# The last normalisation pass of an attention and deformable-convolution kernel: where the second pass over eight results finds its data, and when it is loaded

## What is computed

```python
x = x + attention(group_norm(x))            # 8 heads of 48, 1024 tokens, softmax, projection
x = x + deform(group_norm(x))               # below

offset = clip(conv(x, off_w, off_b), -8, 8)     # 3x3
mask   = 2 * sigmoid(conv(x, mask_w, mask_b))   # 3x3
y      = bilinear samples of x at 9 shifted taps, times mask, times proj_w, plus proj_b
mean, var = y.mean(axis=(0, 2, 3)), y.var(axis=(0, 2, 3))   # over all 8 images
return gelu((y - mean) * rsqrt(var + 1e-5) * gamma + beta)
```

## Time and profile before

| | us |
| --- | --- |
| median of 3 runs | 3541.97 (3540.9 to 3545.35) |
| profiled execution | 3541.39 |
| its span in the trace | 3539.5 |
| PE busy | 3257.9 (92% of the span) |
| DVE busy | 2309.0 (65%) |
| ACT busy | 1672.5 (47%) |
| POOL busy | 1288.1 (36%) |

### The profile page before, as it was taken

One profiled execution on the slowest core, in us unless ns is written; L12 is line 12 of the kernel. 1 busy time (PEld: TensorE's weight loads), 2 busy tenths in 40 slices (PEclk: granted clock), 3 DMA queues, 4 the chain that ended last, 5 costly groups with the idle time before them and its releaser, 6 DMA issues. The chain is left out here.

```text
span 3539.5 us, 87588 instructions
## 1 busy us (share of the span) xinstructions
PE 3257.9 (92%) x33434; PEld 1904.8 (54%) x33434; DVE 2309.0 (65%) x3770; ACT 1672.5 (47%) x2700; POOL 1288.1 (36%) x1183
## 2 busy tenths in 40 slices
PE   5899999999999999999999999999999999997991
PEld 3265555555555555555556555555555555554660
DVE  5976677766766576766767667676676666765443
ACT  4274344544455443744437444464445544363443
POOL 0162334523343332622327133362334423262430
PEclk9799999999999999999999999999999999998995
DMA  4000000000001000000000000000000100001007
GB/s 139 19 2 37 19 1 21 20 19 19 2 22 37 2 19 3 21 37 1 20 21 3 37 19 2 21 2 37 19 1 22 38 1 1 2 21 72 1 1 321
DMA packets 12167, 97.59 MB, mean 28 GB/s; under 512 B 2813, under 2 KB 2941, under 8 KB 5008
## 3 DMA queue, kind: packets, MB, share of 16 engines
q1 hardware_dynamic: 9504, 67.40, 5.1%
q0 software_dynamic: 1152, 12.58, 0.8%
q10 hardware_dynamic: 1008, 11.01, 0.7%
HBM read 56.26 MB, written 34.60 MB: 26 GB/s over the span
## 5 line engine op out<-in xcount | busy, mean ns | idle before, releaser
L1612 PE MATMUL R<-P,WALL 128*128 128x512 f16 x3888 | 980.5, 378 | 0.3 <-issue 0.3
L634 POOL TENSOR_TENSOR PL<-P 128x1024 f16<-128x1024 f32 x256 | 583.0, 2282 | 544.1 <-ACT P L809 541.9
L1051 DVE TENSOR_REDUCE MXP<-G 128x1 f32<-128x512 f32 x926 | 630.7, 688 | 154.4 <-PE G L1368 149.6
L1591 PE MATMUL R<-MHL,XB 128*128 128x240 f16 (+14 forms) x7776 | 719.8, 234 | 2.4 <-DVE P L1282 2.4
L671 POOL TENSOR_TENSOR MHL<-M,MHL 128x280 f16<-128x280 f32 (+2 forms) x576 | 364.8, 635 | 796.3 <-ACT MHL L905 795.1
L809 ACT ACTIVATE P<-R 128x1024 f32<-128x1024 f32 x512 | 521.4, 1023 | 223.7 <-PE R L1413 222.8
L1591 PEld LDWEIGHTS R<-MHL,XB 128*128 128x128 f16 x7776 | 571.1, 98 | 102.5 <-DVE P L1282 2.7
L1612 PEld LDWEIGHTS R<-P,WALL 128*128 128x128 f16 x3888 | 377.9, 98 | 396.7 <-issue 0.5
L1123 DVE TENSOR_TENSOR PL<-P 128x1024 f16<-128x1024 f32 x256 | 463.4, 1812 | 150.8 <-ACT P L809 150.6
L1413 PE MATMUL R<-QK 48*128 48x512 f16 (+1 forms) x3072 | 435.1, 392 | 37.5 <-issue 22.9
L1431 PEld LDWEIGHTS R<-VS,P 128*128 128x128 bf16 x4096 | 322.1, 97 | 196.1 <-issue 155.2
(11 more groups left out here) (146 smaller groups left out, 3535.8 us busy)
## 6 DMA issues: line engine op xcount, KB each, us to landing
XA<-x SPq DMA_DIRECT2D x8, 1536.0 KB, 6.6
X<-x SPq DMA_DIRECT2D x8, 1536.0 KB, 6.8
x_scratch<-X SPq DMA_DIRECT2D x7, 1536.0 KB, 5.8
y_scratch<-XP ACTq DMA_DIRECT2D x7, 1536.0 KB, 5.1
WALL<-y_scratch SPq DMA_DIRECT2D x6, 1536.0 KB, 14.8
out<-WALL POOLq DMA_DIRECT2D x6, 1536.0 KB, 10.9
QK<-x_scratch SPq DMA_DIRECT2D x4, 1536.0 KB, 17.4
P<-wd SPq DMA_DIRECT2D x9, 576.0 KB, 4.9
```

Source lines behind the costliest of these rows:

```text
L634: pool.tensor_tensor(PL[:, s % P_BUFS, :], P32[:, s % P_BUFS, :], high_view(s), ALU.subtract).then_inc(p_low_pool, 1)
L1051: dve.reduce_max(MXP[:, name[1] % 2, n // 2, n % 2:n % 2 + 1], chunk(sec, name)[:, :], AX.X).then_inc(dve_read, 1)
L1591: last = pe.matmul(out, XT[:, x_part, g * BOX_Y + r, t * 128:(t + 1) * 128], MHL[:, m_part, o + at:o + at + (hi - lo) * (x1 - x0)], start= ...
L1612: last = pe.matmul(R6[:, CT + ct, :], WALL[:, w:w + 128], PHL[:, u % 2, part // 2, t, :], start=(u % TAPS == 0 and n < CT), stop=(u % TAPS ...
```

## The change

x1 of all k from 1 to 7 is loaded at about 3224 us, except the last third of the last one, which goes to the first tile of `X1` and waits for the first addition. For this, x1 of 5, 6 and 7 gets places in what the last image no longer needs: the rest of `QK4` and the V weights in `WALL`, `QZ` and `WP`, `WQK` (made flat, `WQKF`) and `X1`.

y of k = 1 and 2 is loaded when `taps_used` is raised, with the convolution of unit 15, after which the weights under these two places are not read again. y of k = 3, 4, 5 and 6 is loaded when `y_full` says that TensorE is through; 3 in `WALL`, the others in `XB`, `P32`, and `PL` with `MHL`. y of k = 7 goes into `YS` after the first result's store. VectorE raises `added` for each tile instead of for each result. GpSimd stores results 0 to 6 as before (6 in two pieces, as its place has two) and result 7 tile by tile.

```diff
+        X_AT = [[X1F], [places(QKF, 0)], [places(QKF, 2 * CT * PIX)], [XR.rearrange("p t n -> p (t n)")],
+                [places(VS[:, :, :, :].rearrange("p q h d -> p (q h d)"), 0)],
+                [places(QKF, 4 * CT * PIX, 2), places(WALL, WVO, 1)], [places(QZF, 0, 2), places(WPF, 0, 1)],
+                [places(WQKF[:, :], 0, 2), X1F[:, 0:PIX]]]
+        Y_AT_END = [[YSF], [places(WALL, 0)], [places(WALL, 4 * CT * PIX)], [places(WALL, 2 * CT * PIX)],
+                    [places(XB[:, :, :, :].rearrange("p a t n -> p (a t n)"), 0)],
+                    [P32[:, 0:CT, :].rearrange("p t n -> p (t n)")], [places(PLF, 0, 2), places(MHLF, 0, 1)], [YSF]]
...
             x1_done(BATCH - 1, True)
-            for k in range(1, min(XS, BATCH)):
-                sp.dma_start(XF(k), x1_d[FINAL[k], :, :]).then_inc(xf_in[k % XS], 16)
-            sp.wait_ge(y_stats, BATCH)
-            if BATCH > 1:
-                sp.wait_ge(y_out, BATCH * 16)
             for k in range(1, BATCH):
-                if k >= 4:
-                    sp.wait_ge(out_done[k % 4], 16 * (k // 4))
-                sp.dma_start(YF(k), y_d[FINAL[k], :, :]).then_inc(yf_in[k % 4], 16)
-                if k >= XS:
-                    sp.wait_ge(added, k - XS + 1)
-                    sp.dma_start(XF(k), x1_d[FINAL[k], :, :]).then_inc(xf_in[k % XS], 16)
+                final_x(k, pieces_of(X_AT[k])[:1 if k == BATCH - 1 else None])
+            sp.wait_ge(y_out, 16 * 3)
+            sp.wait_ge(taps_used, 1)
+            for k in (1, 2):
+                final_y(k)
+            sp.wait_ge(y_out, BATCH * 16)
+            sp.wait_ge(y_full, 2 * BATCH)
+            for k in range(3, BATCH - 1):
+                final_y(k)
+            sp.wait_ge(added, CT)
+            final_x(BATCH - 1, pieces_of(X_AT[BATCH - 1])[1:])
+            sp.wait_ge(out_done[0], 16)
+            final_y(BATCH - 1)
...
+            for k in range(BATCH - 1):
+                pool.wait_ge(added, (k + 1) * CT)
+                for a, cols in pieces_of(Y_AT_END[k]):
+                    pool.dma_start(out[FINAL[k], :, cols], a).then_inc(out_done[k], 16)
+            k = BATCH - 1
+            for t in range(CT):
+                pool.wait_ge(added, k * CT + t + 1)
+                pool.dma_start(out[FINAL[k], :, t * PIX:(t + 1) * PIX], final_tile(Y_AT_END[k], t)).then_inc(out_done[k], 16)
             for k in range(BATCH):
-                pool.wait_ge(added, k + 1)
-                pool.dma_start(out[FINAL[k], :, :], YF(k)).then_inc(out_done[k % 4], 16)
-            for k in range(min(4, BATCH)):
-                pool.wait_ge(out_done[k], 16 * len(range(k, BATCH, 4)))
+                pool.wait_ge(out_done[k], 16 * (CT if k == BATCH - 1 else len(Y_AT_END[k])))
...
-                last.then_inc(added, 1)
+                    dve.tensor_tensor(y, y, final_tile(X_AT[k], t), ALU.add).then_inc(added, 1)
...
                         if u % TAPS == TAPS - 1 and end == CONVS:
                             last.then_inc(y_full, 1)
+                        if final and u == UNITS - 3 and end == CONVS:
+                            last.then_inc(taps_used, 1)
```

More of the change, by code:

```diff
@@ L315, in build @@
         WALL = sb("WALL", [128, (2 * TAPS + 2) * TAPW], fp16)
-        WQK = sb("WQK", [128, 2, CT, 2 * PAIRS, QK_COLS], fp16)
+        WQKF = sb("WQK", [128, 2 * CT * 2 * PAIRS * QK_COLS], fp16)
+        WQK = WQKF[:, :].rearrange("p (a t m n) -> p a t m n", a=2, t=CT, n=QK_COLS)
         WP = sb("WP", [128, 2, CT, CH], fp16)
@@ L437, in build @@
         bn_ready = sem("bn_ready")
-        yf_in = [sem(f"yf_in{n}") for n in range(4)]
-        xf_in = [sem(f"xf_in{n}") for n in range(5)]
+        taps_used = sem("taps_used")
+        yf_in = [sem(f"yf_in{n}") for n in range(BATCH)]
+        xf_in = [sem(f"xf_in{n}") for n in range(BATCH)]
         gelu_done = sem("gelu_done")
         added = sem("added")
-        out_done = [sem(f"out_done{n}") for n in range(4)]
+        out_done = [sem(f"out_done{n}") for n in range(BATCH)]
         count_of = {"F": chunk_full, "A": act_read, "D": dve_read}
@@ L472, in build, with places, pieces_of, final_tile @@
         QKF = QK4[:, :, :, :].rearrange("p a i n -> p (a i n)")
[L473 to L476, removed]
+        X1F, YSF = [a.rearrange("p t n -> p (t n)") for a in (X1[:, :, :], YS[:, :, :])]
         FINAL = [BATCH - 1] + list(range(BATCH - 1))
[L482 to L490, removed]
+        def places(a, first, tiles=CT):
+            return a[:, first:first + 2 * tiles * PIX].bitcast(fp32)
+        WPF = WP[:, :, :, :].rearrange("p a t n -> p (a t n)")
+        QZF, MHLF = QZ[:, :, :, :].rearrange("p a d n -> p (a d n)"), MHL[:, :, :].rearrange("p a n -> p (a n)")
+        X_AT = [[X1F], [places(QKF, 0)], [places(QKF, 2 * CT * PIX)], [XR.rearrange("p t n -> p (t n)")],
[5 more added lines that the diff above has]
+                    [P32[:, 0:CT, :].rearrange("p t n -> p (t n)")], [places(PLF, 0, 2), places(MHLF, 0, 1)], [YSF]]
+        def pieces_of(areas):
+            out, t = [], 0
+            for a in areas:
+                n = a.shape[1] // PIX
+                out.append((a, slice(t * PIX, (t + n) * PIX)))
+                t += n
+            return out
+        def final_tile(areas, t):
+            for a, cols in pieces_of(areas):
+                if cols.start <= t * PIX < cols.stop:
+                    return a[:, t * PIX - cols.start:(t + 1) * PIX - cols.start]
         SELF = SEL[:, :, :].rearrange("p a n -> p (a n)")
@@ L593, in _, with final_x, final_y @@
             x1_done(BATCH - 1, True)
-            for k in range(1, min(XS, BATCH)):
-                sp.dma_start(XF(k), x1_d[FINAL[k], :, :]).then_inc(xf_in[k % XS], 16)
-            sp.wait_ge(y_stats, BATCH)
-            if BATCH > 1:
-                sp.wait_ge(y_out, BATCH * 16)
-            for k in range(1, BATCH):
-                if k >= 4:
-                    sp.wait_ge(out_done[k % 4], 16 * (k // 4))
-                sp.dma_start(YF(k), y_d[FINAL[k], :, :]).then_inc(yf_in[k % 4], 16)
-                if k >= XS:
-                    sp.wait_ge(added, k - XS + 1)
-                    sp.dma_start(XF(k), x1_d[FINAL[k], :, :]).then_inc(xf_in[k % XS], 16)
+            def final_x(k, pieces):
+                for a, cols in pieces:
+                    sp.dma_start(a, x1_d[FINAL[k], :, cols]).then_inc(xf_in[k], 16)
+            def final_y(k):
+                for a, cols in pieces_of(Y_AT_END[k]):
+                    sp.dma_start(a, y_d[FINAL[k], :, cols]).then_inc(yf_in[k], 16)
+            for k in range(1, BATCH):
+                final_x(k, pieces_of(X_AT[k])[:1 if k == BATCH - 1 else None])
[11 more added lines that the diff above has]
+            final_y(BATCH - 1)
         @block.gpsimd
@@ L959, in _ @@
                 if k > 0:
-                    act.wait_ge(yf_in[k % 4], 16 * ((k - 1) // 4 + 1) if k % 4 else 16 * (k // 4))
+                    act.wait_ge(yf_in[k], 16 * len(Y_AT_END[k]))
                 for t in range(CT):
-                    y = YF(k)[:, t * PIX:(t + 1) * PIX]
+                    y = final_tile(Y_AT_END[k], t)
                     act.activation(y, y, ACT.Gelu, bias=BSC[:, 3, t:t + 1], scale=BSC[:, 2, t:t + 1]).then_inc(gelu_done, 1)
@@ L1315, in _ @@
                 if k > 0:
-                    dve.wait_ge(xf_in[k % XS], 16 * ((k - 1) // XS + 1) if k % XS else 16 * (k // XS))
+                    dve.wait_ge(xf_in[k], 16 * len(X_AT[k]))
                 for t in range(CT):
-                    y = YF(k)[:, t * PIX:(t + 1) * PIX]
+                    y = final_tile(Y_AT_END[k], t)
                     dve.wait_ge(gelu_done, k * CT + t + 1)
-                    last = dve.tensor_tensor(y, y, XF(k)[:, t * PIX:(t + 1) * PIX], ALU.add)
-                last.then_inc(added, 1)
+                    dve.tensor_tensor(y, y, final_tile(X_AT[k], t), ALU.add).then_inc(added, 1)
         @block.tensor
```

## The result

| | before | changed |
| --- | --- | --- |
| median, us | 3541.51 (3540.9 to 3545.35, 4 runs) | 3521.63 (3518.61 to 3524.36, 4 runs) |
| ratio | | 0.9944 (95%: 0.9932 to 0.9957) |
| span of the profiled execution | 3539.5 | 3522.5 |
| TensorE's end (ScalarE's first read of the last y) | 3463.00 | 3467.54 |
| from there to the end of the span ("the tail") | 76.5 | 55.0 |

The changed kernel is faster by 0.56%. The profiled execution is its slowest of the four, and that is already in the body: it reaches the last image's x1 loads, the first thing that the change touches, 4.6 us later. The tail is shorter by 21.5 us; 23.5 were forecast.

What follows compares the result with a forecast made beforehand. DMA bytes were taken to bound the end: 17.5 us from fewer transfers, 3.15 from the earlier start and 2.8 of standing still give 23.5 us less, so 3518.5 us, range 3514.5 to 3524.

Steps and rivals of the forecast that it cites:

- The forecast's own part: Whole kernel: the main case without rivals, 3514.5 to 3521 us, chance 0.75.
- the rival in which the last y becomes the chain: Tail: store 0, y7's load, GELU, additions and thirds decide the end; time 3521 to 3524 us, chance 0.15.
- the signs that the forecast named: Changed profile: full DMA share from 3464 to 3514 at 415 to 430 GB/s, TensorE's end at 3463.0 within 0.5 us.
- The end is bound by bytes: Tail: 18 transfers, 28.3 MB at 420 GB/s, take 67.4 us; 4.67 fewer transfers save 17.5 us.
- Loads of x1 at 3224 at no cost: Last image's convolution and first taps: 6.67 loads instead of 4 cost 0, at most 0.2 us.
- the slower rival: Before 3250, 3457 and after 3464: instruction fetches wait behind bulk loads, 37 us lost, time 3555.5, chance 0.03.
- Two y under the taps: Last taps: two y loads issued at 3447.6, landed by 3456.1; cost 0 while covered, 7.5 us without cover.
- The earlier start: TensorE's end: y3 to y6 wait for the last product, not the last statistics; 3.15 us earlier, DMA busy from 3464.0.
- The sum: Tail: 20.97 MB at 420 GB/s is 49.9 us; span 3516.0 against 3539.5, 23.5 us less.
- The last y: Tail: y7, loaded after store 0, takes 12.7 us and lands near 3500; bounds 6.8 and 22.0 us after issue.
- The pieces at 0: Cut transfers in the tail: 18 transfers for 13.33 transfers' bytes cost 0, bounds 0 and 7.5 us; costly-starts rival chance 0.04.
- The thirds of the last store: Kernel's end: first third leaves 2.3 us earlier, but 9.2 us of DMA backlog remain and 2.8 us of standing still vanish.

Runs made afterwards that it cites:

- the second profile: Changed kernel run again, nothing edited, against the kernel before: 3517.10 us against 3539.39, ratio 0.9938, tail 56.2 us.
- the version with the early loads: Changed kernel with y1, y2 loaded earlier, y4, y3, y6 after the last sampling product, y5, y7 in own places: 3510.97 us, ratio 0.9919 to the kernel before.

## Why the prediction held, step by step

The time forecast was 3518.5 us in 3514.5 to 3524; measured were 3521.63 and, in a later comparison, 3517.10. Against the kernel before of the same comparison that is 19.9 and 22.3 us less, where the forecast took off 23.5.

That the first one lies in the range has luck in it. The forecast's own part ended at 3521; up to 3524 the range stood for the rival in which the last y becomes the chain, and that did not happen. What carried the time there is 2 us more of tail and the spread of the body. Of the signs that the forecast named, two did not come as named: TensorE's end moved by 4.5 us, which the second profile shows to be spread, and the DMA engines moved 407 GB/s over 3470 to 3500, under the 415 to 430 expected, if not under 400.

- **The end is bound by bytes.** Right for the changed kernel. The DMA share stays full to the end, with 12 us of stores behind the last issue, and holding that issue back for the whole last result moved the tail by nothing that shows. Taking 2 transfers back made the DMA engines busy 7.2 us longer (7.5 forecast), 2.67 transfers 10.2 us (10.0). Against the kernel before, 4.67 transfers less are 16.9 us less of busy time (17.5 forecast); standing still fell by 4.7 us, from 8.0 to 3.3, where the earlier start and the wait of the last store together were put at 5.95.
- **Loads of x1 at 3224 at no cost.** Right: 238.3 to 239.1 us from their issue to TensorE's end in all thirteen profiles, with four loads (three profiles) and with the long list. That also answers the slower rival, fetches that wait behind bulk, up to TensorE's end: no such hole. Behind it the first GELU stands 7.18 us after TensorE's end, before and after.
- **Two y under the taps.** Right: SP issues them at 3452.25, 4.6 us after the predicted 3447.6, which is the body's shift in that profile, and TensorE stays busy.
- **The earlier start.** Right: the share of 0.76 in 3468 to 3470 puts the first bytes 0.95 us after TensorE's end.
- **The sum.** The tail was forecast as 53.0 (3516.0 - 3463.0) and is 55.0 and 56.2. In both profiles the DMA engines worked 51.5 to 51.6 us (3468.5 to 3520.1 in the first) instead of 49.9. The term that was mis-sized is the rate: 420 GB/s was read from 60 us in the middle, while over its whole tail the kernel before moved its 28.3 MB in 68.5 us of busy time, 414 GB/s, and the changed one its 21.0 MB at 407. Of the first profile's loss, 0.52 MB less than at 420 GB/s is moved between 3482 and 3486, 1.2 us, and 0.27 MB less in the first two microseconds than their share allows, 0.6 us. Such losses are in the traffic of the kernel before too, but spread over more bytes. From 3520.1 to the end of the span are 2.4 us instead of 2.1; the second profile's further 1.2 us are standing still, as said above.
- **The last y.** Landed 11.7 us after its issue, 12.7 forecast; store 0 in 11.3 us. The place in the order was right, and so was that it does not decide here. How near it is was understated: with 2 or 2.67 transfers more in the tail it decides, as the landing grows to 27 and 33 us. The bound of 22.0 us from the rows held for the changed kernel (11.7 and 14.8) and was no bound for those versions.
- **The pieces at 0.** Right in size: 22 more DMAs cost 1.7 to 2.9 us, so the 4.67 extra ones some 0.5 us. The Trainium skill ("DMA: Bandwidth & Descriptors", Rules for kernel authors) asks for 1 MiB or more per DMA for the highest bandwidth; with everything in pieces of 512 KB the tail moved 396 GB/s while the DMA engines were busy, against 407. The Trainium skill ("DMA: Bandwidth & Descriptors", Anatomy of one DMA) also gives a fixed part of about 2.0 us for a DMA that GpSimd issues. An estimate from that figure, paid in series by all 22 (13 are GpSimd's), would be 44 us. Behind a full queue the measurement says 0.1 us each, so here it is not paid in series.
- **The thirds of the last store.** The forecast said that a backlog hides them and that the 2.8 us of standing still vanish. The backlog alone does it: the whole store had the same tail.
- **Not foreseen**: that TensorE's end differs by up to 8.6 us between executions, with the same instructions up to the last image's x1 loads. Single executions of the changed kernel went from 3515.3 to 3524.4, so one alone could have left the range.

## What to carry to other kernels

When the end of a kernel is a saturated stretch of DMA, count the bytes that must move after the last compute result and move every other one under the compute; places come free tile by tile, well before the phase that used them ends, and here earlier loads, three of them between the last sampling product and the last product, each with its own place, took another 8 us off a tail of 55. Cutting transfers into pieces cost little behind a full queue (0.1 us for each DMA more), and cutting the last store gained nothing. Beside the tail, look at how long the DMA engines are busy in it: the two parts, bytes and standing still, answer to different changes. Compare such changes by the stretch from the last product to the end, not by the whole time, since the body's own spread can be nearly half of the gain.

## What the runs showed of the hardware

- Thirteen executions put the end of the same TensorE work between 3458.9 and 3467.5 us, on a granted clock of 0.97 to 0.98 over the span; the last 239 us of it repeat within 0.8 us.
- The last y's 1536 KB, issued after store 0 into a busy DMA stretch, land after 11.7 to 33.1 us; in the slowest case more was ahead of it and beside it. One of the four x1 loads at 3224 landed after 6.8 us.
- After store 0 is issued with 1.6 MB or more of loads still to move, a full DMA share moves little in one or two stretches of 2 us (250 and 328 GB/s in the changed kernel, 307 before), before and after the change. With the loads ended it does not: 295 GB/s at a share of 0.70. It also came once beside loads alone, 356 GB/s at 1.10.
- Stores alone moved 402 GB/s in the version with the early loads and 423 in the changed kernel; loads and stores together 407 over 3470 to 3500, with the slow stretch in it.
- 22 more DMAs of 512 KB in a full stretch of 50 us added 1.5 us of busy time.
